# Reciprocal square roots as powers on GpSimd, and a new order of the steps around them, in a fused convolution and attention kernel

## The reference

```python
x = x + L0(_gn(x), ...)
x = x + L1(_gn(x), ...)

def _gn(v, G=32, eps=1e-05):          # 32 groups of 4 channels
    m, s = mean(g), var(g)            # over a group's channels and positions
    return (g - m) / sqrt(s + eps)

def L0(fmap, ...):
    x = chan_ln(fmap, g_norm)         # over the channels of one position, with rsqrt(var + EPS)
    q, k, v = depthwise3x3(w1 @ x)    # each with its own weights
    q = softmax(q, over 16 channels of a head) * scale
    k = softmax(k, over the 256 positions)
    out = q @ (k.T @ v)               # 8 heads
    return chan_ln(out_w @ silu(out), g_out)

def L1(x, ...):
    qkv = w_qkv @ x
    y = grouped1x1(depthwise5x5(qkv))
    q, k, v = relu, relu, plain of concat(qkv, y)
    out = (v with a row of ones, k) products, divided by their sum
    return w_proj @ out * inv + bias  # inv = bn_gamma / sqrt(bn_var + eps)
```

## Time and profile before

| | |
|---|---|
| median of three runs | 303.05 us |
| profiled execution | 303.94 us, of which the span 302.2 us |
| TensorE matmul, weight load | 253.7 us (84%), 195.3 us (65%) |
| VectorE | 214.7 us (71%) |
| ScalarE | 154.9 us (51%) |
| GpSimd | 115.6 us (38%) |
| mean granted TensorE clock | 0.977 |

### The profile page before, as it was taken

How to read it: one execution, slowest core, us unless ns; L and a number is a source line. 1 busy time by engine, 2 the same in 40 slices (tenths; PEclk the granted TensorE clock), 3 DMA queues, 4 the chain that set the end, 5 groups by cost and what they waited for, 6 DMA issues and landing times. The chain is left out here.

```text
span 302.2 us, 12513 instructions
## 1 busy us (share of the span) xinstructions
PE 253.7 (84%) x5285; PEld 195.3 (65%) x5285; DVE 214.7 (71%) x658; ACT 154.9 (51%) x397; POOL 115.6 (38%) x336
## 2 busy tenths in 40 slices
PE   0448799759799688978579999997899999889994
PEld 0335577549478477767458676775679888566761
DVE  5667587729997447896786867652778888766774
ACT  1356875748973467682437327641343337822320
POOL 8165457307776427764324222230212221333100
PEclk9999999979999999997689999999999999999999
DMA  7620069980001100000003553727000000002212
GB/s 224 141 46 11 0 162 216 220 177 4 4 5 29 44 3 0 3 2 0 0 3 86 130 125 89 181 59 186 5 2 4 4 4 2 2 3 73 72 54 87
DMA packets 15176, 18.61 MB, mean 62 GB/s; under 512 B 3840, under 2 KB 8960, under 8 KB 15120
## 3 DMA queue, kind: packets, MB, share of 16 engines
q1 hardware_dynamic: 13440, 17.23, 23.4%
q10 hardware_dynamic: 1680, 0.58, 0.9%
HBM read 3.54 MB, written 2.20 MB: 19 GB/s over the span
## 5 line engine op out<-in xcount | busy, mean ns | idle before, releaser
L1160 PE MATMUL bank<-cin,tband 64*32 64x240 f32 (+5 forms) x2632 | 82.3, 403 | 5.6 <-DMA cin<-cin 3.2
L1160 PEld LDWEIGHTS bank<-cin,tband 64*32 64x32 f32 x2632 | 67.0, 107 | 19.7 <-issue 4.3
L625 ACT ACTIVATE tband<-tband,row_edge 128x96 f32<-128x96 f32 (+1 forms) x96 | 31.6, 395 | 30.0 <-POOL tband L479 29.1
L1156 PE MATMUL bank<-ident,rings 128*128 128x128 f32 x192 | 32.7, 300 | 15.7 <-ACT rings L577 7.4
L967 DVE STREAM_TRANSPOSE cpos<-bank 64x256 f32<-64x256 f32 x88 | 39.4, 448 | 5.4 <-PE bank L1160 4.2
L1156 PEld LDWEIGHTS bank<-ident,rings 128*128 128x128 f32 x192 | 23.2, 152 | 29.6 <-issue 10.7
L909 DVE STREAM_TRANSPOSE cin<-bank 128x768 f32<-128x768 f32 x32 | 31.0, 976 | 9.9 <-PE bank L1160 9.9
L517 POOL TENSOR_SCALAR ring_v<-cpos,mask_b 128x512 f32<-128x512 f32 x30 | 20.8, 707 | 34.4 <-PE bank L1160 20.9
L577 ACT ACTIVATE rings<-bank,ln_b,ln_s 128x128 f32<-128x128 f32 x64 | 24.3, 472 | 9.2 <-POOL ln_b L454 9.2
L970 DVE STREAM_TRANSPOSE cpos<-bank 128x256 f32<-128x256 f32 x52 | 19.1, 417 | 10.1 <-PE bank L1160 9.9
L479 POOL TENSOR_TENSOR tband<-taps,pw 128x160 f32<-128x160 f32 x24 | 10.6, 460 | 39.9 <-PE bank L1160 39.9
(11 more groups left out here) (146 smaller groups left out, 440.4 us busy)
## 6 DMA issues: line engine op xcount, KB each, us to landing
cin<-cin SPq DMA_DIRECT2D x48, 192.0 KB, 4.1
cin<-cin SPq DMA_DIRECT2D x18, 128.0 KB, 3.4
xin<-in_x_dram SPq DMA_DIRECT2D x4, 512.0 KB, 6.3
out_dram<-rings SPq DMA_DIRECT2D x16, 128.0 KB, 1.8
taps<-tap_rows SPq DMA_DIRECT2D x16, 30.0 KB
taps<-tap_rows SPq DMA_DIRECT2D x16, 18.0 KB
cin<-cin ACTq DMA_DIRECT2D x2, 128.0 KB, 2.8
rings<-in_L_conv_w_qkv_dram SPq DMA_DIRECT2D x1, 192.0 KB, 8.6
```

Source lines behind the costliest of these rows:

```text
L625: last = a.activation(dst[:, :, 1 + e], dst[:, :, 0], ACT.Copy, scale=row_edge[:, e:e + 1])
L1156: last = t_.transpose(tile(dst, xl), src(xl), ident[:, :])
L1160: return t_.matmul(dst, stationary, moving, start=start, stop=stop, skip_group_check=True)
```

## The change

Every reciprocal square root becomes one `tensor_tensor` with the operation `pow` on GpSimd, with a tile of -0.5 as second operand; the chains on GpSimd and on VectorE go. The root of the group norm's lots moves from VectorE to GpSimd. On ScalarE the front's order in a step becomes `xn`, `front_normed`, `xg`, and the attention's order becomes `q_out`, `k_exp`, `z_normed`, `tanh`, `k_out`. On VectorE the statistics of all images stand ahead of the first moments, and the attention's steps have the residual's statistics, `ctx_mask` and `silu` in that order. On TensorE some group means stand one place elsewhere, and the units of pair 0 ahead of the transposes of pair 3.

```diff
@@ gpsimd
+            g.memset(minus_half[:, :], -0.5)
...
-            tap_rows()
-            def rsqrt(dst, w, y, t, before_dst=None):
-                (eleven links)
+            def gn_scale(c, b0, n):
+                pool.wait_ge(s_gnr, c + 1)
+                link(g.tensor_tensor(out=gn_s[:, b0:b0 + n], in0=gvar[:, 0:n], in1=minus_half[:, 0:n], op=ALU.pow))
+                g.tensor_tensor(out=gn_b[:, b0:b0 + n], in0=gtmp[:, 0, 0:n], in1=gn_s[:, b0:b0 + n],
+                                op=ALU.mult).then_inc(s_gn, 1)
             def layernorm(n):
-                rsqrt(scale, w, lnt[:, 0, :], lnt[:, 1, :],
-                      (lambda: pool.wait_ge(s_nrm, n - 1)) if n >= 2 else None)
+                links[0] += 1
+                g.tensor_scalar(less, lmv[:, n % 2, :, 0], -1.0, 1.0, ALU.mult, ALU.mult).then_inc(s_pool, 1)
+                link(g.tensor_scalar(w, lmv[:, n % 2, :, 1], EPS, 1.0, ALU.add, ALU.mult))
+                if n >= 2:
+                    pool.wait_ge(s_nrm, n - 1)
+                link(g.tensor_tensor(out=scale, in0=w, in1=minus_half[:, 0:XL], op=ALU.pow))
                 g.tensor_tensor(out=ln_b[:, n % 2, :], in0=less, in1=scale, op=ALU.mult).then_inc(s_ln, 1)
             def fold_batchnorm():
-                rsqrt(bn_inv[:, :], w, y, t)
+                link(g.tensor_tensor(out=bn_inv[:, :], in0=w, in1=minus_half[:, 0:1], op=ALU.pow))
+            gn_scale(0, 0, B // 2)
+            tap_rows()
             for i in range(PAIRS):
                 layernorm(i)
+                if i == 1:
+                    gn_scale(1, B // 2, B // 2)
...
             for step in range(PAIRS + 4):
...
+                if step == PAIRS + 2:
+                    gn_of_lot(0)
                 if 0 <= step - 4 < PAIRS:
                     layernorm(PAIRS + step - 4)
+            gn_of_lot(1)
             for i in range(PAIRS):
+                if i == 3:
+                    gn_of_lot(2)
@@ scalar, front
             for step in range(PAIRS + 2):
-                if step + 1 < PAIRS:
+                if 0 <= step - 2 < PAIRS:
+                    xn(step - 2)
+                if step == 1:
+                    xg(2)
+                if 0 <= step - 1 < PAIRS:
+                    front_normed(step - 1)
+                if step + 1 < PAIRS and step != 1:
                     if step + 1 == PAIRS // 2:
                         act.wait_ge(s_gn, 2)
                     xg(step + 1)
-                if 0 <= step - 2 < PAIRS:
-                    xn(step - 2)
-                if 0 <= step - 1 < PAIRS:
-                    front_normed(step - 1)
@@ scalar, attention
             def q_out(i):
+                act.wait_ge(s_kq, i + 1)
...
+                if 0 <= step - 1 < PAIRS:
+                    q_out(step - 1)
+                    k_exp(step - 1)
+                if 0 <= step - 5 < PAIRS:
+                    z_normed(step - 5)
                 if 0 <= step - 3 < PAIRS:
                     tanh(step - 3)
                 if 0 <= step - 1 < PAIRS:
-                    q_out(step - 1)
-                if 0 <= step - 5 < PAIRS:
-                    z_normed(step - 5)
-                if 0 <= step - 1 < PAIRS:
                     k_out(step - 1)
-                if step < PAIRS:
-                    k_exp(step)
@@ vector, front
-            gn_scale(0, 0, B // 2)
+            x_stats(B // 2, B - 4)
             dve.wait_ge(s_gn, 1)
             v.tensor_scalar(image3(ring_a[:, 0, :], 1), ...).then_inc(s_xg0, 1)
-            x_stats(B // 2, B - 2)
+            link(x_stats(B - 4, B))
+            gn_aggregate(1, B // 2, B // 2)
             for step in range(PAIRS + 3):
+                if step < PAIRS:
+                    moments(step, bank[X_BANKS[step % 3]][:, :])
+                if step == 0:
+                    gn_variance(1, B // 2, B // 2, bank[7])
+                if step == 1:
+                    gn_read(1, B // 2, bank[7])
...
@@ vector, moments
-                link(last)
-                v.tensor_scalar(lnw[:, n % 2, 0, :], lmv[:, :, 1], EPS, None, ALU.add)
-                v.tensor_scalar(lnw[:, n % 2, 1, :], lmv[:, :, 0], -1.0, None, ALU.mult).then_inc(s_lmv, 1)
+                last.then_inc(s_lmv, 1)
+                dve.wait_ge(s_lmv, n + 1)
@@ vector, attention
+                    x1(step - 6)
                 if 0 <= step - 4 < PAIRS:
-                    moments(PAIRS + step - 4, bank[5 + step % 2][:, :], work, begun)
-                for left in work:
-                    left()
+                    moments(PAIRS + step - 4, bank[5 + step % 2][:, :])
+                if 0 <= step - 6 < PAIRS:
+                    x1_stats(step - 6)
+                if 0 <= step - 2 < PAIRS:
+                    ctx_mask(step - 2)
                 if 0 <= step - 3 < PAIRS:
                     silu(step - 3)
-                if 0 <= step - 2 < PAIRS:
-                    ctx_mask(step - 2)
...
+                if step == GN1[1][2] + 1:
+                    gn_variance_of_lot(1)
...
                         conv_in(p, n, unit(p))
+                        if p == 0 and step == GN1[1][2] + 1:
+                            gn_read_of_lot(1)
+                if step == GN1[2][2]:
+                    gn_variance_of_lot(2)
+                if step == GN1[2][2] + 1:
+                    gn_read_of_lot(2)
                 if 0 <= n - 1 < PAIRS:
                     kv_mask(n - 1)
-                if step == at:
-                    gn_variance(4, 2 * i0, 2 * (i1 - i0), gn_sums[2])
-                if step == at + 1:
-                    gn_read(4, 2 * (i1 - i0), gn_sums[2])
                     attn_div(n - 1)
-                if step == at + 1:
-                    gn_scale(4, 2 * i0, 2 * (i1 - i0))
@@ tensor, front
             for step in range(PAIRS + 3):
+                if step == 3:
+                    front_units(0)
                 if step < PAIRS:
                     transposes of pair step
-                if step - 3 in (0, PAIRS - 2):
+                if step - 3 == PAIRS - 2:
                     front_units(step - 3)
+                if step == 2:
+                    gn_mean(1, 1, B // 2, B // 2, bank[7])
...
-                if step == 1:
+                if step == 0:
                     gn_mean(1, 0, B // 2, B // 2, bank[7])
-                if step == 2:
-                    gn_mean(1, 1, B // 2, B // 2, bank[7])
@@ tensor, block 1
                     units(n, ring_a[:, i % 2, :], w1t, 0).then_inc(s_qkv, 1)
+                    if n == 0 and i == GN1[1][2] + 1 - FRONT1:
+                        gn_of_block1(1, 1)
...
-                if step == GN1[1][2] + 1:
-                    gn_of_block1(1, 0)
                 if 0 <= step - 4 < PAIRS:
                     project(step - 4)
                 if step == GN1[1][2] + 1:
-                    gn_of_block1(1, 1)
+                    gn_of_block1(1, 0)
```

More of the change, by code:

```diff
@@ L816, in _, with link @@
             links = [0]
-            def link(ins, meanwhile=None):
+            def link(ins):
                 links[0] += 1
-                n = links[0]
                 ins.then_inc(s_chain, 1)
-                if meanwhile:
-                    meanwhile.pop(0)()
-                dve.wait_ge(s_chain, n)
-            def rsqrt(dst, n, work=None):
-                w, y, t = newt[:, 0, 0:n], newt[:, 1, 0:n], newt[:, 2, 0:n]
-                link(v.tensor_scalar(y.bitcast(I32), w.bitcast(I32), -0.5, RSQRT_MAGIC, ALU.mult, ALU.add), work)
-                link(v.tensor_tensor(t, y, y, ALU.mult), work)
-                link(v.tensor_tensor(t, t, w, ALU.mult), work)
-                link(v.scalar_tensor_tensor(out=y, in0=t, scalar=N1 / N0, in1=y, op0=ALU.add, op1=ALU.mult), work)
-                link(v.tensor_tensor(t, y, y, ALU.mult), work)
-                link(v.scalar_tensor_tensor(out=t, in0=t, scalar=N0 * N0, in1=w, op0=ALU.mult, op1=ALU.mult), work)
-                link(v.tensor_scalar(w, t, N0 * H0, N0 * H1, ALU.mult, ALU.add), work)
-                link(v.tensor_tensor(t, t, w, ALU.mult), work)
-                link(v.scalar_tensor_tensor(out=dst, in0=t, scalar=N0 * H2, in1=y, op0=ALU.add, op1=ALU.mult), work)
+                dve.wait_ge(s_chain, links[0])
             def small_masks():
@@ L876, in gn_read, with moments @@
                 dve.wait_ge(s_gnp, 2 * c + 2)
-                v.tensor_scalar(newt[:, 0, 0:n], ps[:, B:B + n], EPS, None, ALU.add).then_inc(s_gnr, 1)
-            def gn_scale(c, b0, n, work=None):
-                dve.wait_ge(s_gnr, c + 1)
-                rsqrt(gn_s[:, b0:b0 + n], n, work)
-                v.scalar_tensor_tensor(out=gn_b[:, b0:b0 + n], in0=gtmp[:, 0, 0:n], scalar=-1.0,
-                                       in1=gn_s[:, b0:b0 + n], op0=ALU.mult, op1=ALU.mult).then_inc(s_gn, 1)
-            def tile_stats(n, src, xl):
-                if xl == 0:
-                    if n >= 1:
-                        dve.wait_ge(s_lmv, n)
```

(44 more changed lines are left out.)

64 lines of the change are left out of this document (20 added, 44 removed).

## The result

The changed kernel takes 305.34 us (median of 20 runs, 302.36 to 307.74) where the kernel before, on the same chip, takes 303.14 us (20 runs, 299.83 to 304.91): a ratio of 1.0082, 95% interval 1.0055 to 1.0109. The forecast was 294.8 us. The change does not gain 2.7%, it loses 0.8%. The profiled execution of after took 306.96 us, 1.6 above the median, with a span of 305.2 us. How long TensorE runs at its lower clock level differs from one execution to the next, so what follows compares stretches of the traces more than their ends, and looks for the same stretch in other kernels that have it unchanged.

What follows compares the result with a forecast made beforehand. TensorE was taken to set the end, idling in block 0's front and the first attention behind GpSimd chains. Terms -0.8, -7.1 and -0.4 sum to -8.3 us, giving 294.8 us from a 303.05 median; range 290.8 to 300.8.

Steps and rivals of the forecast that it cites:

- steps 1 to 11: Front of block 0 and first attention, up to block 1's second units: -0.8 and -7.1 us.
- steps 6 and 7: First attention's steps: q's copy no longer behind the tanh, full steps 4.8 for 5.06 us; 1.3 us gained together.
- step 5: Front's copies of cin: start 2.0 us earlier, last release 0.7 later; middle -0.8 us, from -2.0 to +0.7.
- The price of a power: GpSimd power, worked as some 25 passes: 0.4 us for 4 columns, 0.6 for 8, range 0.20 to 3.1.
- step 2: Layernorm 0 in the front: first norm at 18.05 (was 20.82), units 0 at 21.4 instead of 25.93, 4.5 us gained.
- Rivals C and D: C: power is slow scalar routine, 311 us, chance 0.09; D: first power pays one-time code fetch, 297.7 us, chance 0.05.
- Steps 1 and 2: Front's start: first image at 12.85 for 13.46, 0.6 us gained; units 0 start 4.5 us earlier.
- Steps 3 and 4: Front: TensorE slow in units 0; then ScalarE's loop takes 4.65 to 4.7 us a step for 3.76, units 1 at 32.1.
- step 6: First attention, step without back transposition: step 3 loses 0.4 us because q's copy no longer stands behind the tanh.
- Steps 8 to 11: Attention's tail: two layernorms 4.8, clock 1.6, mean 1.5 us gained; new waits for silu 1.3 and variance 0.7 lost.
- step 9: Attention's tail: without the wait ahead, TensorE no longer falls to its slow clock level, 1.6 us gained.
- Step 12: Last group-norm lot: eight VectorE links become one power, 0.8 us gained, variance ahead of masks costs 0.4; -0.4 us.

Runs made afterwards that it cites:

- a4: Kernel after with ScalarE's old orders in both the front and the first attention, all else kept: 294.88 us, ratio 0.9718.
- a1: Kernel after with only ScalarE's order in the first attention put back as before: 298.04 us, ratio 0.9824.
- d4: Kernel after with ScalarE's old attention order, and TensorE's units 1 of the front ahead of pair 4's transposes: 300.13 us, ratio 0.9875.
- a2: Kernel after with the exponential k_exp ahead of the copy q_out in ScalarE's attention step: 300.23 us, ratio 0.9905.
- d1: Kernel after with a separate three-slot buffer for the q tile in block 0's attention, orders unchanged: 296.98 us, ratio 0.9792.
- b2: Kernel before, chains and all, with only ScalarE's new order in the first attention: 308.78 us, ratio 1.0200.
- e3: Kernel before with ScalarE's new attention order and the third slot for q: 304.81 us, ratio 1.0066.
- a3: Kernel after with only ScalarE's order in the front put back as before: 301.16 us, ratio 0.9949.
- b1: Kernel before with only the root chains on GpSimd replaced by powers: 302.22 us, ratio 0.9976.
- c2: Kernel after with both of ScalarE's old orders and the layernorm's power done twice, one result unused: 295.02 us, ratio 0.9766.
- d2: Kernel after with both of ScalarE's old orders and the old chain of eleven instructions in the layernorm: 298.41 us, ratio 0.9851.

## Why the prediction was wrong, step by step

At the second units of block 1 the forecast was -7.9 us (steps 1 to 11) and the profiles show +3.5. Of the 11.4 us between them steps 6 and 7 hold 6.4, step 5 2.8, the convolution's stretch, which no step had, 1.3, and the tail 1.0.

**The price of a power** was 2.5 times too low, 1.02 for 0.4 us, inside the bounds of 0.20 and 3.1. The 25 passes behind the 0.4 stand in no row: measured are 0.156 us a column, which at 1.9 ns a column and pass would be some 80. It is most of the delay of the first norm (19.07 for 18.05 in step 2) and so of the first units (22.42 for 21.4). It is not what made the forecast wrong: a4 has the same power and gains 8.3 us. Rivals C and D did not happen: the point from which a slow power decides was put at 2.85 us, and there was no first-call gap. The Trainium skill's rule of about 6 us at the first call into freshly loaded GpSimd code (GPSIMD Engine Reference, "Instruction dispatch") does not show in this trace: the first power took 1.65 us with no gap ahead of it, and the later one of its size 1.64. Whether anything was freshly loaded for it no run shows.

**Steps 1 and 2** held but for that: the first image at 13.37 (forecast 12.85; the power was not covered), first units 3.5 us earlier.

**Steps 3 and 4.** The loop of 4.65 to 4.7 us was right (4.6). Wrong was the pace: the prediction let TensorE be slow in units 0 only. It had the ramp's wait in its sum (32.1 for units 1), and did not ask what 3.5 us of idle time do to the clock. In after the granted clock is 0.50 from 31 to 37 us, units 2 start at 39.54 where the steps give 36.8, and units 7 at 58.84, not 56 to 57. In a1, with the same front, units 1 start at 32.38, as forecast, and still take 4.49 us. The timeline of a1_old_attn:

```profile
32.38 4.49 PE L1132 MATMUL bank<-w0t,rings 128*32 128x192 f32 x64
...
37.95 22.50 SPq L314 DMA_DIRECT2D cin<-cin  x24
```

The slowness of units 0 is another matter: they take 3.97 to 5.35 us in the 17 profiles while the granted clock is 1.00 from 20 to 30 us in all of them. Its cause stays open.

**Step 5** is the term that was mis-sized for it: -0.8 forecast, +2.0 measured, outside its bounds of -2.0 and +0.7. The middle between two mechanisms was no estimate. In before, after, a1 and a4 the first copy of cin starts at 37.99, 39.67, 37.95 and 34.55, and the convolution 26.0, 26.3, 25.9 and 25.5 us behind it, though units 7 start at 55.57, 58.84, 57.11 and 52.05: a1 has its last units 1.5 us later than before and its convolution no later. So the first alternative held, the copies' backlog hides a late last release; only in d4, where units 7 start at 60.90 behind a first copy at 39.06, is the convolution 29.1 us behind it. What failed is the copies' start: forecast 2.0 us earlier, about 36.0, measured 39.67, since they wait for units 1, which ran at the slow pace. And the 2.0 us are one execution. The four profiles with after's front (after, a1, a2, d1) start the convolution at 65.95, 63.80, 66.79 and 64.41, the three with the front of before (before, b2, e3) at 63.99, 63.38 and 63.31: 1.7 us later in the mean.

**Steps 6 and 7 are what failed most.** The prediction said of step 6 that "the copy of q no longer stands behind the tanh" and counted it a gain. It did not look at what the copy waits for: two slots for q, so that the copy of pair s-1 waits for the attention product of pair s-3, of the same step. In the old order the tanh of pair s-3 stood ahead and waited for that product anyway; the wait was free. At the head of the step it holds the exponential, the norm and the tanh, and through silu and the projection the next attention product. Forecast -1.3 us by the end of step 7, measured +5.1, of which 4.1 stand in both other profiles with this order and two slots (a3, b2). Shown three ways: undoing the order (a1, -7.3 us), the order alone on the old kernel (b2, +6.1), a third slot (d1, -8.4). The 4.8 us a step that were forecast are what the order gives with the slot, 4.65; that the shorter layernorm brings them was wrong too, since b1, c2 and a4 have 5.02 to 5.03 with one power or two.

**Steps 8 to 11** were right in sum. From the transposes of pair 7 to the second units after takes 24.5 us, 4.9 less than before; in a1 and a4, where the steps' loop does not reach into the tail, the same stretch is 22.8, 6.5 less, of which 4.8 + 1.6 + 1.5 - 1.3 - 0.7 = 5.9 were forecast. The clock in the tail is 1.00 (step 9); the waits for silu are 1.19 and 1.96 us, 3.15 where 1.3 was forecast, and the variance's 0.73 (forecast 0.7). **Step 12**: after keeps at the end of the span 3.0 of the 3.5 us of the second units, -0.5 for -0.4; a1 and a4 gain the same 0.5 there. That a4 as a whole gains 8.3 us, just the forecast's sum, is chance: it has ScalarE's old orders and steps of 5.03, not 4.8.

The chances: of what was given to slower, 0.09 went to a slow power and 0.02 to a small loss without a mechanism. The new order on ScalarE in the attention had none, though the runs make it the dearest part of the change.

## What to carry to other kernels

Before an instruction moves to the head of an engine's step, list what it waits for and at which point of the same step that is produced; with a ring of two slots the consumer may be this very step, and then everything behind it joins a loop. A wait is free only behind another wait for the same thing, and work placed ahead of a wait is free where work behind it is not. When a reorder leaves an engine idle for some microseconds during a ramp, cost the clock behind the gap as well as the gap. And try the parts of a mixed change apart: here the parts were worth +7, +4 and -8 us, and one more tile of buffer turned the worst of them into a shorter step (4.65 for 5.03), though beside the old chains (e3) it still left a loss of 0.7%.

## What the runs showed of the hardware

A power on GpSimd costs 0.55, 1.02, 1.32 and 1.64 us for 1, 4, 6 and 8 columns of 128 partitions, against about 0.20 for an ordinary operation on four columns: some 0.39 us and 0.156 more a column.

TensorE's granted clock fell to 0.50 during or behind 3.49 us of idle time in the front of after, a1, a2 and d1, and the 64 unit matmuls behind it took 4.49 to 4.82 us. Behind idle stretches of 2.14 and 3.50 us (d4) and 2.57 us (d2) they took 4.39 to 4.49, behind 1.64 or 1.65 us in the eleven other profiles 2.81. The first 64 of the front took 3.97 to 5.35 us at a granted clock of 1.00. At the convolution's start the granted clock is below 1.00 in 16 of 17 profiles, before and the fastest kernel included, and 1.00 only in e3.
